# A two-layer transformer on one core: the set-up of weights, gates and modulations in another order

## The reference

```python
# layer 0
gamma1 = cond @ g1_w + g1_b; beta1 = cond @ b1_w + b1_b      # gamma2, beta2 likewise
alpha1 = tanh(cond @ a1_w + a1_b) * 0.1                      # alpha2 likewise
y = layernorm(x, ln1_g, ln1_b) * (1 + gamma1) + beta1
x = x + attention(y, qkv_w, proj_w) * alpha1
z = layernorm(x, ln2_g, ln2_b) * (1 + gamma2) + beta2
x = x + (gelu(z @ fc1_w + fc1_b) @ fc2_w + fc2_b) * alpha2
# layer 1: shift, scale = split(cond @ ada_w + ada_b); rotary q and k; mask; no gates
```

## Time and profile before

| | |
|---|---|
| profiled execution, its own time | 1885.72 us |
| its span, first to last instruction | 1883.9 us |
| TensorE busy | 1788.1 us (95%) |
| TensorE weight loads busy | 1637.1 us (87%) |
| ScalarE busy | 1306.7 us (69%) |
| VectorE busy | 1237.4 us (66%) |
| GpSimd busy | 849.4 us (45%) |
| granted clock, mean | 0.986 |

### The profile page before, as it was taken

How to read it: one execution, slowest core, us unless ns; L and a number is a source line. 1 busy time by engine, 2 the same in 40 slices (tenths; PEclk the granted TensorE clock), 3 DMA queues, 4 the chain that set the end, 5 groups by cost and what they waited for, 6 DMA issues and landing times.

```text
span 1883.9 us, 41740 instructions
## 1 busy us (share of the span) xinstructions
PE 1788.1 (95%) x12623; PEld 1637.1 (87%) x12623; DVE 1237.4 (66%) x2985; ACT 1306.7 (69%) x2327; POOL 849.4 (45%) x1036
## 2 busy tenths in 40 slices
...
GB/s 166 107 147 95 100 97 133 117 128 111 97 96 119 122 122 122 89 105 108 124 149 109 84 108 98 98 107 114 84 86 105 101 103 106 103 84 97 93 71 34
DMA packets 330276, 199.84 MB, mean 106 GB/s; under 512 B 160995, under 2 KB 314597, under 8 KB 330213
## 3 DMA queue, kind: packets, MB, share of 16 engines
...
## 4 chain that ended last, share of the span: by engine, by line
PE 73%; DVE 12%; issue 8%; SPq 2%; ACT 2%; DMA 1%; POOL 1%; DVEq 0%; POOLq 0%; ACTq 0%
PE D L1106 17%; PE C L912 16%; PE B L912 9%; PE B L1064 9%; PE A L1031 7%; PE B L1050 5%; PE A L912 5%; PE E L912 4%; DVE mx L1373 2%; SPq L329 2%; DVE o_sb L1397 2%; PE A L1036 2%; DVE exps L1379 1%; DVE ot_lo L1406 1%; PE E L1075 1%
## 5 line engine op out<-in xcount | busy, mean ns | idle before, releaser
L559 POOL TENSOR_TENSOR h_lo<-hact,h_hi 128x512 fp32r<-128x512 f32 x256 | 330.4, 1291 | 302.6 <-ACT h_hi L762 289.5
L1031 PE MATMUL A<-k_pad,q_pad 128*128 128x256 f32 x1536 | 259.9, 296 | 14.3 <-DVE exps L1379 9.3
L1106 PE MATMUL D<-wgt_hi,h_hi 128*128 128x256 f32 x1024 | 263.4, 290 | 0.0
L771 ACT COPY probs_turned<-B 128x512 f32<-128x512 f32 x256 | 147.7, 584 | 157.7 <-PE B L1050 157.7
L1064 PE MATMUL B<-v_blocks,probs_turned 128*128 128x68 f32 x2048 | 255.8, 272 | 0.4 <-ACT probs_turned L771 0.4
L1106 PE MATMUL D<-wgt_lo,h_hi 128*128 128x256 f32 x1024 | 255.7, 282 | 0.0
L1064 PEld LDWEIGHTS B<-v_blocks,probs_turned 128*128 128x128 f32 x2048 | 250.3, 193 | 5.8 <-ACT probs_turned L771 2.5
L757 ACT ACTIVATE hact<-C,b_col 128x512 f32<-128x512 f32 x256 | 176.1, 688 | 96.0 <-PE C L912 92.1
L1031 PEld LDWEIGHTS A<-k_pad,q_pad 128*128 128x128 f32 x1536 | 214.8, 194 | 18.3 <-issue 9.5
L1373 DVE TENSOR_REDUCE mx<-A 128x8 f32<-128x512 f32 x256 | 174.3, 681 | 69.3 <-PE A L1036 39.4
L766 ACT ACTIVATE exps<-exps 128x512 f32<-128x512 f32 x256 | 160.9, 630 | 76.3 <-DVE exps L1379 75.7
...
## 6 DMA issues: line engine op xcount, KB each, us to landing
k_pad<-k_flat SPq DMA_DIRECT2D x512, 64.0 KB, 2.1
q_pad<-q_flat SPq DMA_DIRECT2D x256, 128.0 KB, 2.3
gates<-gates SPq DMA_DIRECT2D x64, 256.0 KB, 4.5
...
rotation<-rotation SPq DMA_DIRECT2D x256, 64.0 KB, 1.9
...
gates<-gated_bias SPq DMA_DIRECT2D x32, 256.0 KB, 5.0
...
```

The costliest lines, as they stand in the source:

```text
L559: pool.tensor_tensor(hb[1][:, m % 2, :], hact[:, m % 2, :], hb[0][:, m % 2, :].bitcast(F32), ALU.subtract).then_inc(h_lo, 1)
L1031: ins = nc.tensor.matmul(dst, qpad[g % 2][:, c, p, b, :, :].rearrange("p x s -> p (x s)"), kpad[g % 2][:, c, q, :, b * S:(b + 1) * S], sta ...
L1106: ins = nc.tensor.matmul(Dk[g // 2][:, (g % 2) * D:(g % 2 + 1) * D], hb[p][:, m % 2, g * P:(g + 1) * P], w_slice(q, W_FF2, D, m, 0, D), st ...
```

## The change

The arithmetic is the same and its results go where they went. What moves:

- **SyncE.** In `begin` the mask and qkv come behind the first columns, then a1, a2, g2, b2, then the qk bias loads, proj, the bias rows, the v and fc1 columns and the second columns. fc2 is loaded behind the spreads of step -1, ahead of the gate rows; fc1, the two ada matrices and their columns behind the spreads of groups 2 and 3 in step 0 (`modulation_weights`). Layer 1's 16 qk bias loads come at the end of step 1 (`layer_columns`), and the other biases, the rotary table and the layer's qkv and proj at the end of step 14 (`layer_weights`, eleven loads). In step -1 the first group's queries are spread before the second group's keys. The gated bias of tile 0 is read at the end of step 0.
- **TensorE.** The gate products and the turning of the mask (`gate_products`) stand in step -1 behind the turning of tile 0; the 32 products of layer 1's modulation stand in step 0 behind the first values of tile 1. The first modulation products no longer wait for the columns.
- **ScalarE.** qkv is converted before it waits for the first modulation; tanh and proj's conversion are in step -1; fc2 and fc1 are converted in eight pieces spread over step 0.
- **VectorE.** The low parts of q and k are made between y's shift and y_low, and v's after it (`low_values`), then the gates (`gate_parts`); the second modulation is in step 0 behind the fourth subtract; the low pieces of fc2 stand around `low_qk` in step 0, those of fc1 at its end; the 16 operations of layer 1's modulation are in step 1 behind `z_shift` of the second pair. The waits for `bias_in[1]` are at the start of step 15.
- **GpSimd.** The memsets of k_pad come before the first rstd.
- ada's second matrix goes to the third part of the gates buffer and the first to the third part of the rotation buffer.

The diff, cut to what changes:

```diff
@@ -176,7 +176,9 @@
 w_in = [sem("w_qkv_in"), sem("w_proj_in"), sem("w_ff1_in"), sem("w_ff2_in")]
+cols_in = [sem("cols1_in"), sem("cols2_in"), sem("ada_cols_in")]
 bias_in = [sem("bias0_in"), sem("bias1_in")]
+mask_out, w_lo_v, bias_rows_in = sem("mask_out"), sem("w_lo_values"), sem("bias_rows_in")
@@ -373,46 +375,52 @@
         ld(mods_in[0], mod_raw[n], rows(w[0][m + "_w"]))
-    columns(mods_in[0], 0, 0, [w[0]["g1_b"], w[0]["b1_b"]])
+    columns(cols_in[0], 0, 0, [w[0]["g1_b"], w[0]["b1_b"]])
+    ld(mask_in, mask_u8[:, :], t["mask_BxS_bf1"])
     ld(w_in[0], qkv, rows(w[0]["qkv_w"]))
-    qk_columns(0, [w[0]["qkv_b"][0:2 * D]])
-    other_columns(0, w[0]["qkv_b"][2 * D:3 * D], w[0]["fc1_b"])
-    projection(0, w[0]["proj_w"])
...
         ld(gates_in, gate_row[:, n, :], row(w[0][m + "_b"]))
-    ld(gates_in, bias_rows[:, 0, :], w[0]["proj_b"].partition_broadcast(P))
-    ld(gates_in, bias_rows[:, 1, :], w[0]["fc2_b"].partition_broadcast(P))
...
         ld(mods_in[1], mod_raw[2 + n], rows(w[0][m + "_w"]))
-    columns(mods_in[1], 0, 1, [w[0]["g2_b"], w[0]["b2_b"]])
-    ld(w_in[2], w_raw[1].rearrange("p (k n) -> p k n", k=KC), rows(w[0]["fc1_w"]))
+    qk_columns(0, [w[0]["qkv_b"][0:2 * D]])
+    projection(0, w[0]["proj_w"])
+    ld(bias_rows_in, bias_rows[:, 0, :], w[0]["proj_b"].partition_broadcast(P))
+    ld(bias_rows_in, bias_rows[:, 1, :], w[0]["fc2_b"].partition_broadcast(P))
+    other_columns(0, w[0]["qkv_b"][2 * D:3 * D], w[0]["fc1_b"])
+    columns(cols_in[1], 0, 1, [w[0]["g2_b"], w[0]["b2_b"]])
...
+def second():
     ld(w_in[3], w_raw[2].rearrange("p (k n) -> p k n", k=MC), rows(w[0]["fc2_w"]))
-    ld(mask_in, mask_u8[:, :], t["mask_BxS_bf1"])
...
-def second():
...
         ld(rows_out, gbias[n], gbias_rows[:, n, :])
-    sp.wait_ge(mask_made, 3)
-    ld(rows_out, mask_rows, mask_add)
-    sp.wait_ge(rows_out, 80)
-    sp.wait_ge(mod_done, 16)
...
-def third():
...
-    sp.wait_ge(w_lo[2], 4)
+    sp.wait_ge(rows_out, 64)
+    sp.wait_ge(pe_mods, 2)
...
+def modulation_weights():
...
+    ld(w_in[2], w_raw[1].rearrange("p (k n) -> p k n", k=KC), rows(w[0]["fc1_w"]))
+    sp.wait_ge(pe_gates, 1)
...
         ld(mods_in[2], ada_raw[n], rows(w[1][f"ada{n + 1}_w"]))
-        columns(mods_in[2], 1, n, [w[1][f"ada{n + 1}_b"][D:2 * D], w[1][f"ada{n + 1}_b"][0:D]])
+        columns(cols_in[2], 1, n, [w[1][f"ada{n + 1}_b"][D:2 * D], w[1][f"ada{n + 1}_b"][0:D]])
...
+def third():
+    sp.wait_ge(pe_mods, 4)
...
+def layer_columns():
...
+def layer_weights():
...
     sp.wait_ge(w_lo[0], 1)
+    sp.wait_ge(w_lo_v, 1)
@@ -443,6 +451,12 @@
+def gated_bias(u):
+    wait_apart(sp, sp_passed, (x1_moved, upto(u, 16, 0)))
+    for h in range(2):
+        sp.dma_start(x1b[h * S:(h + 1) * S, :, :], gbias_tiles[1][u, h].partition_broadcast(S))\
+          .then_inc(gbias2_in, 16)
@@ -460,6 +474,8 @@
         spread_queries(u, 3)
+    if known(u) and u == 0:
+        modulation_weights()
@@ -476,13 +492,8 @@
         sp.dma_start(x_in, tokens_of(u + 2, n)).then_inc(x_loaded, 16)
-    if b == 0:
-        wait_apart(sp, sp_passed, (x1_moved, upto(u, 16, 0)))
-        if known(u) and u == 0:
-            wait_apart(sp, sp_passed, (w_lo[3], 4))
-        for h in range(2):
-            sp.dma_start(x1b[h * S:(h + 1) * S, :, :], gbias_tiles[1][u, h].partition_broadcast(S))\
-              .then_inc(gbias2_in, 16)
+    if b == 0 and not (known(u) and u == 0):
+        gated_bias(u)
@@ -496,15 +507,28 @@
         swap(u + 1, 3)
+    if known(u) and u == -1:
+        wait_apart(sp, sp_passed, (mask_made, 3))
+        ld(mask_out, mask_rows, mask_add)
...
         spread_keys(u + 1, 0)
-        spread_keys(u + 1, 1)
+        if not (known(u) and u == -1):
+            spread_keys(u + 1, 1)
...
         spread_queries(u + 1, 0)
+        if known(u) and u == -1:
+            spread_keys(u + 1, 1)
         spread_queries(u + 1, 1)
+    if known(u) and u == 0:
+        wait_apart(sp, sp_passed, (w_lo[3], 4))
+        gated_bias(0)
+    if known(u) and u == 1:
+        layer_columns()
+    if known(u) and u == NT - 2:
+        layer_weights()
@@ -518,9 +542,9 @@
     pool.wait_ge(sem_ident, 3)
-    first_rstd(0)
...
         pool.memset(buf[...].bitcast(F32), 0.0).then_inc(pad_zero, 1)
+    first_rstd(0)
@@ -676,23 +700,15 @@
     first_norm(0)
+    high_weights(0, 0)
...
     first_columns(0, 0)
-    high_weights(0, 0)
-    act.wait_ge(bias_in[0], NBIAS[0])
...
 def second():
-    high_weights(1, 0)
-    act.wait_ge(pe_gates, 1)
-    nc.scalar.activation(hact[:, 1, :], C[:, :], ACT.Tanh).then_inc(gates_tanh, 1)
-    for n in (2, 3):
-        for q in range(MC // 2):
-            high_piece(n, 0, q)
-    act.wait_ge(mod_done, 16)
+    pass
...
 def third():
-    act.wait_ge(mod_done, 32)
-    act.wait_ge(bias_in[1], NBIAS[1])
+    pass
@@ -778,6 +794,8 @@
 def step(u, n, a, b, c, p):
+    if known(u) and u == NT - 1:
+        act.wait_ge(bias_in[1], NBIAS[1])
@@ -817,24 +835,38 @@
         hidden_high(u - 1, 1)
+    elif known(u) and u == 0:
+        high_piece(3, 0, 0)
+        high_piece(3, 0, 1)
...
         first_high(u + 1, 1)
+    if known(u) and u == -1:
+        act.wait_ge(pe_gates, 1)
+        nc.scalar.activation(hact[:, 1, :], C[:, :], ACT.Tanh).then_inc(gates_tanh, 1)
+        high_weights(1, 0)
+        act.wait_ge(bias_in[0], NBIAS[0])
...
         hidden(u - 1, c, 2)
+    elif known(u) and u == 0:
+        high_piece(3, 0, 2)
...
         hidden_high(u - 1, 2)
+    elif known(u) and u == 0:
+        high_piece(3, 0, 3)
...
         hidden(u - 1, c, 3)
+    elif known(u) and u == 0:
+        high_piece(2, 0, 0)
...
@@ -893,9 +931,13 @@
         high_piece(2, 1, 2)
+    if known(u) and u == NT - 2:
+        act.wait_ge(mod_done, 32)
...
         first_columns(u + 2, n)
+    if known(u) and u == 0:
+        act.wait_ge(mod_done, 16)
@@ -932,36 +974,29 @@
     pe.wait_ge(cond_turned, 1)
-    pe.wait_ge(mods_in[0], 16 * 6)
+    pe.wait_ge(mods_in[0], 16 * 2)
...
-def second():
+def gate_products():
+    pe.wait_ge(mask_made, 3)
+    nc.tensor.transpose(E[:, 0:P], mask01[:, :, :].rearrange("p a s -> p (a s)"), ident[:, :])\
+        .then_inc(pe_mask, 1)
     pe.wait_ge(consts_ready, 2)
-    pe.wait_ge(gates_in, 16 * 6)
+    pe.wait_ge(gates_in, 16 * 4)
...
     ins.then_inc(pe_gates, 1)
-    pe.wait_ge(mods_in[1], 16 * 6)
...
+def second():
+    pe.wait_ge(mods_in[1], 16 * 2)
     modulations(Dk[1], mod_raw[2], mod_raw[3])
-    pe.wait_ge(mask_made, 3)
-    nc.tensor.transpose(E[:, 0:P], mask01[:, :, :].rearrange("p a s -> p (a s)"), ident[:, :])\
-        .then_inc(pe_mask, 1)
     pe.wait_ge(mask_turned, 1)
-    pe.wait_ge(w_lo[1], 1)
-    pe.wait_ge(pad_zero, 4)
...
 def third():
-    pe.wait_ge(mods_in[2], 16 * 10)
-    pe.wait_ge(mod_done, 16)
-    for n in range(2):
-        modulations(Dk[n], ada_raw[n][:, :, D:2 * D], ada_raw[n][:, :, 0:D])
-    pe.wait_ge(mod_done, 32)
     pe.wait_ge(gates_tanh, 1)
-    pe.wait_ge(w_lo[2], 4)
-    pe.wait_ge(w_lo[3], 4)
@@ -1008,6 +1043,8 @@
         pe.wait_ge(pv_norm, upto(tile - 1, 2 * G, 7 + pair))
+    if known(tile) and tile == 0:
+        pe.wait_ge(w_lo_v, 1)
@@ -1076,16 +1113,16 @@
 def project(u, g):
-    if g == 0 and known(u) and u == NT:
-        pe.wait_ge(w_lo[1], 2)
+    if g == 0 and known(u) and u % NT == 0:
+        pe.wait_ge(w_lo[1], u // NT + 1)
...
 def hidden(tile, m):
-    if known(tile) and tile == NT and m % 2 == 0:
-        pe.wait_ge(w_lo[2], 4 + m // 2 + 1)
+    if known(tile) and tile % NT == 0 and m % 2 == 0:
+        pe.wait_ge(w_lo[2], 4 * (tile // NT) + m // 2 + 1)
@@ -1093,8 +1130,10 @@
 def back(tile, m):
-    if known(tile) and tile == NT and m % 2 == 0:
-        pe.wait_ge(w_lo[3], 4 + m // 2 + 1)
+    if known(tile) and tile % NT == 0 and m % 2 == 0:
+        pe.wait_ge(w_lo[3], 4 * (tile // NT) + m // 2 + 1)
+    if known(tile) and tile == 0 and m == 0:
+        pe.wait_ge(mod_done, 32)
@@ -1144,6 +1183,8 @@
         first_turn(u + 1, 1, b)
+    if known(u) and u == -1:
+        gate_products()
@@ -1190,6 +1231,11 @@
         values(u + 1, a, 0, b)
+    if known(u) and u == 0:
+        pe.wait_ge(mods_in[2], 16 * 2)
+        pe.wait_ge(mod_done, 16)
+        for n in range(2):
+            modulations(Dk[n], ada_raw[n][:, :, D:2 * D], ada_raw[n][:, :, 0:D])
@@ -1215,13 +1261,18 @@
     if n == 0:
-        for kind in W_PIECES:
...
+        for kind in W_PIECES[1 - layer:]:
...
+def low_values():
+    nc.vector.tensor_tensor(qkv_piece("v", wgt[1], True), qkv_piece("v", w_source(0, 0), False),
+                            qkv_piece("v", wgt[0], True).bitcast(F32), ALU.subtract).then_inc(w_lo_v, 1)
@@ -1254,14 +1305,18 @@
         nc.vector.memset(buf[...].bitcast(F32), 0.0).then_inc(pad_zero, 1)
+    dve.wait_ge(mask_in, 16)
+    nc.vector.tensor_scalar(mask_add, mask_u8[:, :], BIG, -BIG, ALU.mult, ALU.add).then_inc(mask_made, 1)
+    for n in range(2):
+        nc.vector.tensor_copy(mask01[:, n, :], mask_u8[:, :]).then_inc(mask_made, 1)
```

(69 more changed lines are left out.)

## The result

The changed kernel takes 1878.22 us (median of 7, 1875.63 to 1880.13), the kernel before 1885.76 (median of 7). The ratio is 0.9961, 95% interval 0.995 to 0.9972: 7.5 us faster, where 16.5 were forecast. Its profiled execution took 1880.13 us with a span of 1878.3, so the two traces are 5.6 us apart, less than the medians.

What follows compares the result with a forecast made beforehand. TensorE was taken to bound the bulk, in-order waiting the first 114 us. A 20.7 us gain at step 1's start, less 3.2 (step 1), 0.5 (its columns) and 0.5 (step 14), gave 16.5: 1869 us, range 1862 to 1877.

Steps and rivals of the forecast that it cites:

- Step 0: what is late next: SyncE waits for gate rows behind fc2 before group 2's spreads; scores start at 46 instead of 59.05, gain left 13.0 us.
- Set-up: Up to step 0's first maximum: earlier products at the upper clock bring it to 31.0 from 51.21, gain 20.2 us.
- Behind group 2: Rest of step 0 runs as before; VectorE's inserted low pieces of fc2 cost 0.6 us in all (bounds 0 and 2).
- The 32 products: Layer 1's modulation products on TensorE in step 0, near 78, delay the last heads and values by 4.1 us.
- Step 0 to step 1: Low pieces of fc1 take 2.5 us plus 1.5 for meeting GpSimd; step 1 starts at 93.5, gain 20.7.
- Step 1: VectorE's sixteen modulation operations delay TensorE's turning of heads by 3.2 us (bounds 2.5 and 5).
- The lower clock at step 1's start stays: At step 1's start TensorE still waits for VectorE and keeps the lower clock; 1 us back if not.
- Step 14: Layer 1's loads start behind the last spread; wv lands 0.5 us after ScalarE wants it (bounds 0 and 2.5).
- Rival 2: Set-up and step 0: the DMA queue stays late, bias loads hold conversions, step 0 gains 6, not 13; 1876, chance 0.20.
- Rivals 1: Step 0: SyncE is no new bound, rows land in 1.8 us, group 2's scores start at 43; 1864, chance 0.16.
- 3: Rival 3, step 0: TensorE's layer 1 products wait for their loads and the gap only moves; 1883, chance 0.04.
- 4: Rival 4, step 14: layer 1's eleven loads land one after another, 12 us slower; 1898, chance 0.04.

Runs made afterwards that it cites:

- e1: The changed kernel with fc2 issued behind step 0's spreads instead of in front of the gate rows: 1874.21 us.
- e2: The changed kernel with group 2's spreads issued before SyncE waits for the rows and issues the gates, fc2 still in front of the rows: 1872.10 us.
- e3: The changed kernel with both edits of SyncE's order, fc2 behind step 0's spreads and group 2's spreads in front of the gates: 1869.83 us.
- e5: The changed kernel with 18 products of the identity on TensorE behind the gate products, to keep it busy ahead of q and k: 1877.33 us.
- e4: The changed kernel with layer 1's eleven loads of step 14 issued in SyncE's idle time instead of behind the last spread: 1879.63 us.
- e6: e3 with layer 1's 32 modulation products and VectorE's 16 operations moved from steps 0 and 1 to between the two steps: 1868.46 us.
- e7: e3 with eight of VectorE's 16 operations for layer 1 moved from step 1 to its idle time at step 0's end: 1865.93 us.
- e10: The changed kernel with only one edit, eight of layer 1's 16 operations moved to VectorE's idle time at step 0's end: 1874.91 us.
- e8: The changed kernel with both SyncE orders, eight operations moved to step 0's end, early loads in step 14 and 18 identity products: 1863.32 us.

## Why the prediction was right and where it was wrong

The direction was right, and so was where the time would come from: the set-up's stalls and the gap between steps 0 and 1. The size was 9 us off, outside the range. The trace, 11.0 short at the end (5.5 for 16.5), has it by terms: 3.7 are missing at the first maximum, 2.4 more at group 2's scores and 2.6 more at the last aggregate of step 0; 1.6 come back between the steps; 0.4 go in step 1, 1.3 in step 14 and 2.2 behind it. So 8.7 of the 11.0 are lost by the end of step 0.

**The step that failed is "Step 0: what is late next".** It named the right engine and mechanism, SyncE and the rows behind fc2, and mis-sized its time. The forecast had the rows issued by 33.7 and landed at 38; they were issued by 38.1 and landed at 42.58, so the wait was 4.4 us as forecast, at a place 4.4 us later. The spreads of group 2 then took 4.5 us of issue instead of 4.0, and the last landed 2.3 behind its issue instead of 1.5. Scores of group 2: 52.23 instead of 46, a gain of 6.8 instead of 13.0. e1, e2 and e3 show that this order was worth 4.0, 6.1 and 8.4 us. That e3 ends at 1869.83, the forecast's number, is in part luck: its order is not the forecast's, its group 2 starts at 44.31 and not 46, and step 0 behind that costs more than forecast (25.2 us to group 3's first maximum, for 22.4). The bounds of that step (43.5 to 50) were too narrow because they let only the landing vary, not the time at which SyncE comes to the rows.

**Why SyncE came late.** Of the 4.4 us: the first product 0.8 late (18.93 for 18.1), two products at the lower clock 1.6, two spreads of q that took 2.80 of issue instead of 1.35 (1.4), and the rest in fc2 and the rows. The clock was on the list as a risk (first scores 2.8 later, "kept for the range"), and the text took the upper level for 1.8 us of idleness; there were 2.55. So "Set-up" failed too, by taking the upper level without a row that showed it. In e5 with 31.20 for the first maximum, and by chance in e1 with 30.86, the clock stays and the spread of q takes 1.34; with the short spread and the lower clock it comes at 32.9 to 34.0 (e3, e4, e6, e7, e10).

**Behind group 2: mis-sized again.** From group 2's scores to group 3's first maximum step 0 took 25.5 us, against 21.8 before; 0.6 was forecast for the inserted pieces. 2.1 of the 3.7 go with TensorE at the lower clock behind its 6.67 us of waiting: scores take 1.65 instead of 0.96 and weighing 1.81 instead of 1.11, and the heads of group 1 are multiplied 11.9 us behind the scores instead of 9.7. Another 1.0 stands between tile 1's first product and group 3's maximum (9.9 for 9.0), where ScalarE and VectorE have their inserted pieces and TensorE waits 0.98 for a move that stands behind two high pieces of ScalarE. The full clock alone would not have brought the 21.8: e3, e7 and e8 have it at group 2 and took 25.2, 23.9 and 25.9, since VectorE there waits 1.92, 1.16 and 2.5 us for the residual (see e3). How the 1.0 divides between the pieces of ScalarE and those of VectorE was not tried.

**The 32 products** cost 3.55 us (forecast 4.1), both groups of 16 passes at 1.95 us, in the place named, though near 88 and not 78. That is the lengthening from group 3's first maximum to the last aggregate.

**Step 0 to step 1.** The low pieces took 2.46 as forecast. The 1.5 us for GpSimd did not come. The Trainium skill, GPSIMD Engine Reference, section Specifications, speaks of contention on the shared interfaces; this trace agrees that there is some, but here GpSimd's three small operations are slowed (0.47, 0.87 and 0.69), and x1_bias starts only behind the low pieces. In e6 the same pair met the other way round, and VectorE lost 1.7 us.

**Step 1.** The size was right (4.0, for 3.2 with bounds 2.5 and 5), its reason half of it. The forecast had VectorE's operations delay the turning of heads; e7 and e10 show that half of them can go and with them 4.4 to 5.2 us, more than all 16 had cost. By their windows the lower clock behind TensorE's idleness was part of the price, and some of it had been there before the change (0.71 and 0.65 in the first 16 us of step 1). "The lower clock at step 1's start stays" missed that it would come twice.

**Step 14** cost 1.8 (0.5 forecast, within its bounds of 0 to 2.5): wv landed 4.6 behind its issue, as the forecast took it from the earlier trace rows, but it was issued at 883.56, 3.1 before ScalarE came to its conversion, and not 4.1. e4's trace won all of it back.

**The rivals.** Rival 2 gave 1876 and "6 in place of 13" for step 0, which is what was measured (6.8), and stands nearest to the result. Its cause is not what happened: no bias load held the first conversion, and fc2 landed in 6.2 us, not 11.1. Rivals 1, 3 and 4 fell: the rows took over 5 us, the gap went, and the loads of step 14 overlapped.

**The rule on ring order.** The rows took 5.6 and 5.3 us with fc2 in front and 2.0 and 1.8 without (e1). The Trainium skill, DMA: Bandwidth & Descriptors, section Queues, rings and completion order, has descriptors consumed in ring order on each DMA engine; these numbers agree with it.
